# A graph network's key one-hots: shifting a half visit's keys by the group's offset before they are compared

## The reference

```python
edge_index = jnp.stack([src, dst])
h = jnp.maximum(_layernorm(x, axis=-1), 0.0)
x = x + _L0_gnn_ref(h, edge_index, edge_attr_64, edge_weight, ...)   # edge MLP, messages, segment_sum
h = jnp.maximum(_layernorm(x, axis=-1), 0.0)
x = x + _L1_gnn_ref(h, edge_index, W1, b1, W2, b2)

def _L1_gnn_ref(x, edge_index, W1, b1, W2, b2):
    src, dst = (edge_index[0], edge_index[1])
    agg = jax.ops.segment_sum(x[src], dst, num_segments=x.shape[0])
    h = x + agg
    h = jax.nn.relu(h @ W1 + b1)
    h = h @ W2 + b2
    return jax.nn.relu(h)
```

## Time and profile before

| | us |
|---|---|
| median of 3 runs (lowest, highest) | 3265.5 (3261.2, 3267.5) |
| the profiled execution, its own time | 3264.75 |
| its span | 3262.9 |
| PE busy, DVE busy, POOL busy in the span | 2507.4, 1661.6, 2180.5 |
| counting stage, about 2195 to 3200 | 1005 |

### The profile page before, as it was taken

The page is one execution under the profiler, slowest core; times in us unless marked ns, Lnnn a source line. Parts: engine busy times, 40 slices in busy tenths (PEclk is TensorE's granted clock), DMA queues, the critical chain, the costliest instruction groups (busy, mean ns, idle before and its releaser), DMA issues.

```text
span 3262.9 us, 55219 instructions
## 1 busy us (share of the span) xinstructions
PE 2507.4 (77%) x15482; PEld 1659.5 (51%) x15483; DVE 1661.6 (51%) x3557; ACT 946.1 (29%) x941; POOL 2180.5 (67%) x2231
## 2 busy tenths in 40 slices
PE   3777787778878787878787777627788888888888
PEld 2555555555555565555555655522444454444445
DVE  5533333333333333333333333388877778777783
ACT  3333333333333333233333333231222222222221
POOL 2677777777777777777777777427566766666662
PEclk8888888888888888888889888657999898998999
DMA  5344444444444444444444444312222222222222
GB/s 175 112 128 129 129 127 129 130 125 129 128 131 124 131 125 130 127 130 129 128 129 129 129 129 129 62 71 68 57 60 59 67 61 61 64 60 66 60 66 63
DMA packets 185156, 341.45 MB, mean 105 GB/s; under 512 B 83611, under 2 KB 95388, under 8 KB 184960
## 3 DMA queue, kind: packets, MB, share of 16 engines
q0 software_dynamic: 80896, 165.82, 19.8%
q1 hardware_dynamic: 104162, 174.71, 15.3%
HBM read 329.06 MB, written 11.26 MB: 104 GB/s over the span
## 4 chain that ended last, share of the span: by engine, by line
POOL 29%; PE 23%; issue 21%; DVE 14%; DVEq 8%; DMA 4%; ACT 0%; POOLq 0%; SPq 0%; ACTq 0%; PEldq 0%
POOL big L470 29%; DVE arena L1142 6%; PE ps L655 5%; PE ps L666 5%; PE ps L745 4%; DMA big<-table,idx 4%; PE ps L760 2%; PE ps L646 2%; DVEq L1127 2%; DVE arena L1139 2%; DVE big L958 2%; DVEq L943 2%; DVEq L1142 1%; DVEq L1139 1%; PE ps L638 1%
## 5 line engine op out<-in xcount | busy, mean ns | idle before, releaser
L470 POOL DMA_INDIRECT big<-table,idx x2208 | 2157.1, 977 | 951.9 <-issue 671.5
L958 DVE TENSOR_TENSOR big<-ps,big 128x1024 f32<-128x1024 f32 x196 | 240.0, 1225 | 1250.5 <-DMA big<-table,idx 1247.1
L542 ACT ACTIVATE big<-big 128x1024 f32<-128x1024 f32 x196 | 207.2, 1057 | 1343.1 <-DVE big L958 1343.1
L745 PE MATMUL ps<-arena 128*128 128x500 bf16 x1416 | 416.1, 417 | 146.7 <-DVE arena L1142 145.6
L1142 DVE TENSOR_SCALAR arena<-iota_k,win_off,arena 128x500 bf16<-128x500 f16 x1416 | 500.3, 406 | 0.0
L666 PE MATMUL ps<-hot,big 128*128 128x64 f32 x3136 | 479.9, 307 | 7.6 <-DVE acc L951 7.6
L655 PE MATMUL ps<-wn1b,arena 128*128 128x128 f32 x1568 | 270.0, 343 | 258.3 <-DVE big L958 258.3
L666 PEld LDWEIGHTS ps<-hot,big 128*128 128x128 f32 x3136 | 461.0, 225 | 7.7 <-ACT big L542 7.7
L646 PE MATMUL ps<-arena,we 128*128 128x512 f32 x784 | 436.6, 684 | 3.9 <-ACT arena L532 3.9
L655 PEld LDWEIGHTS ps<-wn1b,arena 128*128 128x128 f32 x1568 | 249.1, 250 | 338.5 <-issue 333.5
L655 PE MATMUL ps<-wn1b,ef 128*128 128x128 f32 x1568 | 223.5, 301 | 172.1 <-DVE big L958 172.1
(11 more groups left out here) (140 smaller groups left out, 1918.5 us busy)
## 6 DMA issues: line engine op xcount, KB each, us to landing
arena<-in_ew SPq DMA_DIRECT2D x196, 512.0 KB
arena<-in_ea SPq DMA_DIRECT2D x196, 256.0 KB, 2.8
big<-table,idx POOLq DMA_INDIRECT x2208, 2.5
table<-big SPq DMA_DIRECT2D x7, 672.0 KB, 3.0
idx<-in_src SPq DMA_DIRECT2D x276, 4.0 KB, 1.6
xs<-in_x SPq DMA_DIRECT2D x7, 448.0 KB, 8.3
table<-nodes SPq DMA_DIRECT2D x7, 448.0 KB, 2.5
out<-xs SPq DMA_DIRECT2D x7, 448.0 KB, 2.5
```

The source lines that it names most:

```text
L470: pool.indirect_dma_start(to(u, q, t), None, table, bass.IndirectOffsetOnAxis(ap=idx[:, u, at:at + 1], axis=0))\
L745: m = pe.matmul(p_c[i % 2], hot_src[:, t, :], hot_key[:, t, :], start=False, stop=True, skip_group_check=True)
L958: dve.tensor_tensor(msg[:, u % 2, :, :, :].rearrange("p q t d -> p (q t d)"), p_pre2, rows[:, u, :, :, :].rearrange("p q t d -> p (q t d)" ...
```

## The change

Each half of a visit gets an instruction ahead of its wait for `c_hot_free`: it subtracts the window's offset from the two to four keys of the half and writes them to a small new tile `key_rel` (128 x 2 x 4, one part for each half), and raises a new semaphore `key_shifted`. Each L1142 (now L1148) compares `iota_k` with one column of `key_rel` at a fixed address: one operation and one per-partition scalar in place of two. The first one of each half waits for `key_shifted`, since an instruction doesn't otherwise wait for what the one before it on the same engine wrote. The matmuls, buffers and DMAs are as before.

```diff
--- before.py
+++ after.py
@@ -166,6 +166,7 @@
         iota_b = sb("iota_b", [P, P], F16)
         iota_k = sb("iota_k", [P, CK], F16)
         zeros = sb("zeros", [1, CK], BF16)
+        key_rel = sb("key_rel", [P, 2, VH])
         rel = sb("rel", [P, NTILE])
         idx = sb("idx", [P, RING, 2 * TB], I32)
         RROW = RING * 2 * TB * D
@@ -286,6 +287,7 @@
         win_loaded = sem("win_loaded")
         src_loaded = sem("src_loaded")
         c_hot = sem("c_hot")
+        key_shifted = sem("key_shifted")
         c_hot_free = sem("c_hot_free")
         c_built = sem("c_built")
         c_moved = sem("c_moved")
@@ -1134,14 +1136,17 @@
                     made = dve.snap(seen, min_val=0, max_val=NWIN * MAX_VISITS * 2)
                     n = VTS[i] // 2
                     for h in (0, 1):
+                        dve.tensor_scalar(key_rel[:, h, 0:n], key_all[:, h * n:NTILE + VT][:, bass.ds(at, n)],
+                                          win_off[:, bass.ds(win, 1)], None, ALU.subtract).then_inc(key_shifted, 1)
                         dve.wait_ge(c_hot_free, made + (h + 1))
                         half_src = src_b_all[:, h * n:NTILE + VT][:, bass.ds(at, n)].rearrange("p (t a) -> p t a", a=1)
                         dve.tensor_tensor(hot_src[:, h * VH:h * VH + n, :], iota_v.to_broadcast([P, n, P]),
                                           half_src.to_broadcast([P, n, P]), ALU.is_equal)
                         for t in range(n):
-                            m = dve.tensor_scalar(hot_key[:, h * VH + t, :], iota_k[:, :], win_off[:, bass.ds(win, 1)],
-                                                  key_all[:, h * n + t:NTILE + VT][:, bass.ds(at, 1)],
-                                                  ALU.add, ALU.is_equal)
+                            if t == 0:
+                                dve.wait_ge(key_shifted, made + (h + 1))
+                            m = dve.tensor_scalar(hot_key[:, h * VH + t, :], iota_k[:, :], key_rel[:, h, t:t + 1], None,
+                                                  ALU.is_equal)
                         m.then_inc(c_hot, 1)
                     dve.reg_add(seen, seen, 2)
```

## The result

| | median us | lowest, highest | runs |
|---|---|---|---|
| before | 3263.35 | 3260.18, 3267.5 | 4 |
| after | 3369.91 | 3365.66, 3372.73 | 4 |

The ratio is 1.0321 (1.0307 to 1.0335): the change makes the kernel 3.2% slower, some 106.6 us. The forecast was 3345 with a range of 3290 to 3392.

What follows compares the result with a forecast made beforehand. DVE's sequencer was taken to set the end of small windows, with PE's pace near it (2.27 against 2.44 us). 86 us lost there and -6 in large windows gave +80 on 3264.75, so 3345, range 3290 to 3392.

Steps and rivals of the forecast that it cites:

- The mechanism: Counting stage: the wait for key_shifted holds DVE's sequencer; 3345 us, range 3310 to 3390 including D, chance 0.80.
- second-half term: Small window's second half: the held sequencer reaches L1151 0.4 us later, 0.26 after L1143's start instead of 0.15 ahead.
- first-half term: Next window's first half: four more sequencer steps of 0.06 us before L1143 is issued, estimated at 0.25 us.
- small window: Windows i = 5 to 11, two-tile halves, 133 in all: 2.27 us becomes 2.92, 86 us together.
- lower end: Total if the scalar's price is double, the second operation counting too: about +45 us, 3310.
- price of the scalar: Each comparison L1142: 62 ns less, 404 to about 344 ns, 88 us of engine time over 1416.
- windows i = 0 to 4: Large windows: the added 0.65 us falls into existing waits and some engine gain stays, counted as -6 us.
- PE's wait for L1148: Sign of being right in the counting stage: this wait goes up from 145.6 us by 60 or more.
- B: Rival, DVE's queue: the sequencer is not held, small windows change about nothing, large ones gain; 3253 us, chance 0.10.
- C: Rival, small windows: sequencer held but PE's pace covers it, +20 to +30 us, 3290; chance 0.06.
- D: Rival, TensorE's clock: lower-level stretches spread over small windows, up to +40 us more, 3385; chance within the main case's 0.80.
- E: Rival, whole kernel: all effects cancel, 3265 us; chance 0.04.

Runs made afterwards that it cites:

- e2w: The changed kernel with comparisons reading a constant tile and the shift behind the c_hot_free wait, wait for key_shifted kept: 3378.52 us, ratio 1.0357.
- e2n: e2w without the wait for key_shifted, the 518 shifts still running: 3278.04 us, ratio 1.0048 to the kernel before.
- e6: Kernel before, with L1139 raising key_shifted and each half's last comparison to wait for it: 3969.97 us, ratio 1.0115, on a chip where before takes 3924.58.
- e1: Kernel before, comparisons reading only the key through a register address, window's offset left out, no shift or wait: 3232.72 us, ratio 0.9914.
- e2z: e2n without the 518 shifts, leaving one-scalar comparisons at a fixed address: 3212.12 us, ratio 0.9846 to the kernel before.
- e4: Changed kernel with one shift for both halves of a window's first visit, outside the loop, wait only in its first half: 3220.72 us, ratio 0.9869.
- e8: e5 with the range checks of the block base loads left out too: 3179.05 us, ratio 0.9742 to the kernel before.
- e5: e4 without the window entry's range check, later visits told by comparing the entry with a constant: 3198.3 us, ratio 0.981.

## Why the prediction was right, and where it was off

**The mechanism.** The wait on DVE's own earlier instruction holds its sequencer, and the register work of what comes next loses its lead. Shown by e2w against e2n (100 us for the wait alone, all of it "issue" in DVE's idle time), and by the place of L1151 in all visits; e6 adds that a held sequencer costs time without any shift. The second-half term was 0.40 us a window. Over the small windows the median start of L1151 against the second half's L1143 is 0.14 after, where before it was 0.16 ahead: 0.30. The 0.12 that I had put in for issuing two one-hots isn't there: L1151 starts 0.05 after the shift's end. The first-half term was 0.25; from the start of L1133's register operation to L1143 it takes 0.63 instead of 0.37: 0.25. A small window grew from 2.27 to 2.84 in the rows shown. The 38 windows i = 7 and i = 10, which have neither `pair_hots` nor `add_sums1` with them, grew from 2.28 to 3.00 in the median and from 2.38 to 2.97 in the mean, with 2.92 forecast.

**Slips in the sum.** By its own premise (PE needs 2.44 us, so only what goes beyond 0.17 counts) a small window had 0.48 to lose, 64 us in all; the sum charged the whole 0.65, 86 us. The measured windows side with the whole. The lower end is off by its own numbers too: as much down as up is 80 - 42 = 38 us, 3303, and not 45 and 3310. And DVE's busy time in the stage rose by 21 us, as forecast, by luck: the comparisons saved 68 us instead of 88, the shifts took 133 instead of 109, and overlap hid the difference.

**The price of the scalar.** 62 ns forecast; L1148 has a median of 344 ns against 404. No run takes the scalar away without its operation, so the 60 ns are the price of both together. The Trainium skill's figures ("VectorE: DVE Perf Modes", "The TRN2 errata"), read as saying nothing of a scalar, would have left it unchanged. Engine time saved and kernel time saved are two things, though: of the 88 us forecast, 29 were gained without the wait (e1), or 48 with the register instruction (e2z).

**The mis-sized term: windows i = 0 to 4.** I counted -6, "the added 0.65 falls into waits that exist". Taken from each window's first half to the next one's, over the 19 batches, the windows i = 5 to 11 grew by 76 us (86 forecast) and i = 0 to 4 by 28, most of it at i = 2 to 4 (5.6, 13.0 and 9.1), where visits have three-tile halves. The waits that I counted on were there, but they were waits for PE, and the sequencer took PE's place as the last to arrive: ahead of three-tile halves DVE stood idle for 32.4 us, 30.0 of them for PE, and now for 24.0 + 16.9 = 41 us, 23.9 of them "issue". In the windows i = 2 to 4 as a whole, idle time that ended with PE fell from 32 to 22 us and idle time that ended with "issue" grew from 1 to 37. Of that, 11 us stand ahead of `add_sums1`, a place that the sum didn't look at. Over the stage "issue" ended 57.0 us of idle time there (L1086), and in the waits of before it was:

```profile
DVE acc L1084 <- issue: 22.9, 29, 1.2
```

So a three-tile window, which I had put with the eight-tile ones, belonged to the small ones. The whole sum was 80 for 106.6, of which this term is 34 too little and the small windows 10 too much; the other 2 to 3 us lie outside the windows. That the total is only 27 us off is in part luck, as the two errors have opposite signs.

**A sign that failed.** PE's wait for L1148 was to grow by 60 or more and grew by 48. The loss is there in another form: L747 itself is 22.7 us longer, and the row sums L762 another 25 (150.1 + 141.6 against 136.8 + 130.0 us in their two groups). 48 and 48 together are most of the 106 us. In these runs, where PE stands idle more it is granted the lower clock for longer (0.91 without the wait, 0.86 with it), and part of what would be a wait becomes slower matmuls.

**The rivals.** B, the sequencer isn't held: refuted at its own point, since L1151 starts after the shift has ended, and by e2w against e2n. One variant is left by the experiments. Between the waiting comparison and L1151 stands at least one more comparison, and it could be this one that finds no place behind the waiting one and holds the sequencer. Only L1016, with nothing between it and the waiting L1009, speaks for the waiting instruction itself. The diagram in the Trainium skill ("Perfetto Trace Analysis", "DVE / Act Engine Instruction") doesn't describe what these traces show for a wait on the engine's own instruction; L1016 was the right row to go by. C, PE's pace covers it: refuted, the loss is 106.6 us and not 20 to 30, and DVE's wait for PE fell from 88.4 to 32.2. D, the clock: its sign is right (0.92 to 0.86), its share open, as said under e2w. E, all cancels: refuted by the time.

## What to carry over

When an engine's idle time ends with "issue", read its sequencer's rows: what counted in this loop is how far ahead the register, branch and load instructions run, and here a wait on the engine's own instruction ended that lead. So a small producer is issued once and early, into a tile that takes turns, and the wait for it goes where much other work still lies behind it and ahead of the loop's end (e4: the same idea, 3220.72 us against 3369.91 as it was tried). When you count waits that are to swallow an added delay, ask of each size of window who would arrive last then, and not only whether there is a wait.

## What the hardware did that I had not expected

- A shift of 2 to 4 elements takes 257 ns in the mean (median 228, 209 to 449), against 0.21 us forecast from a one-element instruction. From its start to the start of the next it is 0.13 us where the one-hot is issued right behind it (2785.35 to 2785.48).
- The same saving in the comparisons was worth 86 to 89 us with the wait and 48 without. That the held sequencer makes what is behind it dearer is the likely reason, not a tested one.
- Range checks of the loads count in this loop: e8 against e5 is 19 us for the base loads' checks alone.
- Chips differ more than the change does: 3924.58 us for the kernel before on one, 3260 to 3263 on others. Why isn't known.
